# Norms and logits of the first experts stage moved into the last steps of the attention before it, with one program instead of three

## The reference, cut to what matters

```
x = x + tanh(g_xattn[0]) * L0_xattn(layernorm(x), ctx)
# L0_ffn, on h = layernorm(x):
probs = softmax(h @ Wr.T)                      # 8 experts
top 2 of probs, scaled to sum 1 -> w[t, e]
mid = einsum('ti,eri->ter', h, A)              # rank 16 for each expert
lora = einsum('ter,te,eor->to', mid, w, Bm) * 2.0
x = x + tanh(g_ffn[0]) * (h @ Wb.T + bias + lora)
x = x + tanh(g_xattn[1]) * L1_xattn(layernorm(x), ctx)   # with an RMS norm in front
```

## Time and profile before

| | us |
|---|---|
| median of 3 runs (lowest, highest) | 1671.79 (1670.3, 1673.09) |
| the profiled execution, its own time | 1676.02 |
| span of its trace | 1673.8 |
| last project of the first attention, last matmul starts | 160.63 |
| first logits matmul of the experts stage | 168.20 |
| first dense matmul | 184.49 |
| first kv matmul of the second attention | 220.99 |

### The profile page before, as it was taken

How to read it: one execution, slowest core, us unless ns; L and a number is a source line. 1 busy time by engine, 2 the same in 40 slices (tenths; PEclk the granted TensorE clock), 3 DMA queues, 4 the chain that set the end, 5 groups by cost and what they waited for, 6 DMA issues and landing times.

```text
span 1673.8 us, 25566 instructions
## 1 busy us (share of the span) xinstructions
PE 1552.4 (93%) x8786; PEld 1231.5 (74%) x8786; DVE 900.1 (54%) x1793; ACT 699.6 (42%) x2010; POOL 633.3 (38%) x602
## 2 busy tenths in 40 slices
PE   5897978988879999999999999899899999999998
PEld 4664766657668888888888887677677777777775
DVE  5786557858831221222222223688666766776666
ACT  4443244436435444543444344553334434333442
POOL 3543135466433231331323132334544444454430
PEclk9998999989999999999999999899999999999998
DMA  5000111011120110101001010104321212212001
GB/s 208 1 2 25 52 45 38 1 57 68 45 76 26 39 51 1 64 15 37 26 27 51 1 51 30 59 34 112 93 72 51 89 39 77 64 54 74 29 14 51
DMA packets 27885, 81.41 MB, mean 49 GB/s; under 512 B 3248, under 2 KB 11952, under 8 KB 22768
## 3 DMA queue, kind: packets, MB, share of 16 engines
q1 hardware_dynamic: 26896, 79.44, 14.4%
q10 hardware_dynamic: 864, 0.30, 0.1%
HBM read 69.25 MB, written 10.49 MB: 48 GB/s over the span
## 4 chain that ended last, share of the span: by engine, by line
PE 52%; issue 12%; DVE 4%; POOL 3%; ACT 1%; POOLq 0%; DVEq 0%; ACTq 0%
PE bank L397 32%; PE bank L1296 7%; PE bank L1284 2%; PE pair L2082 2%; PE bank L2060 2%; PE pair L1265 2%; POOL wo_low L388 1%; PE pair L397 1%; PE bank L1273 1%; POOL wq_low L1021 1%; PE bank L2068 1%; POOL probs L1030 1%; DVE probs L1914 0%; DVE out_low L1944 0%; DVE small L222 0%
## 5 line engine op out<-in xcount | busy, mean ns | idle before, releaser
L397 PE MATMUL bank<-hid_high,wq_high 128*128 128x512 f32 (+1 forms) x640 | 257.6, 402 | 1.7 <-issue 1.5
L397 PE MATMUL bank<-hid_high,wq_low 128*128 128x512 f32 (+1 forms) x640 | 239.9, 375 | 0.0
L397 PE MATMUL bank<-hid_low,wq_high 128*128 128x512 f32 (+1 forms) x640 | 238.5, 373 | 0.0
L1206 DVE SCALAR_TENSOR_TENSOR x_stream<-bank,gates,x_stream 128x512 f32<-128x512 f32 x64 | 48.1, 751 | 352.8 <-PE bank L1296 352.8
L1030 POOL TENSOR_TENSOR probs<-probs,small 128x512 f32<-128x512 f32 x64 | 67.1, 1048 | 356.9 <-DVE small L1194 356.9
L1809 ACT ACTIVATE probs<-probs,small 128x64 f32<-128x64 f32 x256 | 86.2, 338 | 135.2 <-DVE small L1933 135.2
L397 PEld LDWEIGHTS bank<-hid_high,wq_high 128*128 128x128 f32 x640 | 122.9, 192 | 25.5 <-issue 4.6
L397 PEld LDWEIGHTS bank<-hid_high,wq_low 128*128 128x128 f32 x640 | 122.7, 192 | 22.8 <-issue 0.2
L397 PEld LDWEIGHTS bank<-hid_low,wq_high 128*128 128x128 f32 x640 | 123.5, 193 | 20.3 <-issue 3.1
L1104 ACT ACTIVATE probs<-pair,small 128x128 f32<-128x128 f32 x256 | 90.5, 366 | 82.8 <-DVE small L1188 80.2
L593 POOL TENSOR_TENSOR probs<-probs,small 128x512 f32<-128x512 f32 x64 | 66.8, 1043 | 127.8 <-DVE small L773 127.6
(11 more groups left out here) (339 smaller groups left out, 4012.7 us busy)
## 6 DMA issues: line engine op xcount, KB each, us to landing
raw_q<-in_L_wq SPq DMA_DIRECT2D x18, 1024.0 KB, 4.9
raw_o<-in_L_wo SPq DMA_DIRECT2D x18, 1024.0 KB, 4.9
values<-ctx_values SPq DMA_DIRECT2D x32, 256.0 KB, 4.0
values_t<-ctx_keys SPq DMA_DIRECT2D x8, 512.0 KB, 3.3
raw_c<-in_L_wkv SPq DMA_DIRECT2D x6, 512.0 KB, 3.5
raw_o<-in_L_wkv SPq DMA_DIRECT2D x5, 512.0 KB, 4.8
x_stream<-in_x SPq DMA_DIRECT2D x8, 256.0 KB, 9.9
ctx_keys<-raw_o SPq DMA_DIRECT2D x8, 256.0 KB, 2.0
```

The lines of the kernel that those rows point to most:

```text
L397: last = k.nc.tensor.matmul(out, stationary(a, c), moving(b, c), start=n == 0, stop=n == total - 1)
L1206: nc.vector.scalar_tensor_tensor(xt, k.bank[7][:], gate, xt, ALU.mult, ALU.add).then_inc(k.x_done, 1)
```

## The change

The blocks of `attention_first`, `experts` and `attention_second` become one block, and `experts` is gone. In its place:

- Within the steps of the first attention: tile t is normalized and transposed in step `DENSE_SLOT[t]` (25, 27, 29, 31, 33, 34, 35 for tiles 0 to 6), and its low part and its logits come one step later. The statistics of tiles 0 to 6 are taken one tile at a time, with POOL's power right in its steps. ACT splits the experts' weights in steps 23 (`wc`) and 24 to 27 (`wq`), POOL in steps 24 and 25 (`wc`) and 26 to 29 (`wq`). The choice among experts for tiles 0 to 3 is in DVE's steps 34 (`choose`) and 36 (`weigh`).
- `dense_tail`: tile 7's norm and logits, the choice for tiles 4 to 7, the dense and second products of all tiles, the updates.
- The second attention follows without a barrier; its weights are fetched as soon as the buffers are free.
- The buffers of `mid`, tables and second weights move to places that the first attention has done with.

```diff
+DENSE_SLOT = {0: 25, 1: 27, 2: 29, 3: 31, 4: 33, 5: 34, 6: 35}
+DENSE_AT = {n: t for t, n in DENSE_SLOT.items()}
...
     # attention16, POOL, step n
+            if not rms:
+                if n == 8:
+                    dense_clear()
+                if n % 4 == 2 and n >= 10:
+                    dense_rstd(n // 4 - 2)
+                if n in (24, 25):
+                    dense_low_c(n - 24)
+                if 26 <= n < 30:
+                    dense_low_q(n - 26)
...
     # attention16, ACT, step n
+            if not rms and n - 2 in DENSE_AT:
+                logits(DENSE_AT[n - 2])
...
+            if not rms:
+                if n == 23:
+                    high_c()
+                if 24 <= n < 28:
+                    high_q(n - 24)
+                if n in DENSE_AT:
+                    high(DENSE_AT[n])
+                if n == 35:
+                    exponent(0)
...
     # attention16, DVE, step n
+            if not rms and n - 1 in DENSE_AT:
+                low(DENSE_AT[n - 1])
+            if not rms and n in DENSE_AT:
+                apply(DENSE_AT[n])
...
+            if not rms and n == 34:
+                choose(0)
+            if not rms and n == 36:
+                weigh(0)
...
     # attention16, PE, end of step n
+            if not rms and n in DENSE_AT:
+                dense_transposes(DENSE_AT[n])
+            if not rms and n - 1 in DENSE_AT:
+                dense_logits(DENSE_AT[n - 1])
...
     # dense_tensor
+    def transposes(t):
         pe.wait_ge(k.route_xn, t + 1)
         if t:
             pe.wait_ge(k.route_lo, t)
...
+    def logits(t):
         pe.wait_ge(k.route_lo, t + 1)
         if t:
             pe.wait_ge(k.route_sbuf, t)
         else:
+            pe.wait_ge(k.lo_c, k.at("lo_c", 4))
...
+    # dense_tail
+    @block.vector
+    def _(dve):
+        tile_stats(7, k.at("x_done", 0))
+        scale_bias(k.at("loaded_const", 0))
+        apply(7)
+        low(7)
+        choose(1)
+        update(0)
+        weigh(1)
+        update(1)
+        next_stats(0)
+        for t in range(2, T):
+            update(t)
+            next_stats(t - 1)
+
+    @block.tensor
+    def _(pe):
+        dense(0)
+        transposes(7)
+        dense(1)
+        gated(0)
+        logits(7)
+        dense(2)
+        second(0)
+        second(1)
+        second(2)
+        dense(3)
+        second(3)
+        gated(1)
+        for t in range(4, T):
+            dense(t)
+            second(t)
...
-def attention_second(k):
-    with k.nc.Block() as block:
+        dense_tail(k, block)
         attention16(k, 1, True, block)
         quant_mlp(k, block)
```

More of the change, by code:

```diff
@@ L567, in _ @@
             ln_rstd_gpsimd(k, pool, p, p + 1 - k.early)
+        for p in range(LATE if rms else 0):
+            ln_rstd_gpsimd(k, pool, p, p - 2)
         last_rstd_gpsimd(k, pool)
@@ L668, in _ @@
         queries(0, 1)
-        for n in range(N + LAG + 1):
+        if not rms:
+            high_c, high_q, high, logits, exponent, gated = dense_scalar(k, act)
+        for n in range(N + LAG + 1 if rms else N + LAG + 2):
             d = n - LAG
+            if not rms and n - 2 in DENSE_AT:
+                logits(DENSE_AT[n - 2])
             if 0 <= d < N:
@@ new lines, in choose @@
+    def choose(b):
+        dve.wait_ge(k.route_sbuf, k.at("route_sbuf", 4 * b + 4))
+        rows = slice(4 * b, 4 * b + 4)
+        top, lg, cut, rep, wgt = (m[n][:, rows] for n in ("top", "lg", "cut", "rep", "wgt"))
+        for t in range(4):
+            last = nc.vector.max(top[:, t, :], lg[:, t, 0:8])
+        chain.step(last)
+        nc.vector.tensor_tensor(wgt, lg[:, :, 0:8], top[:, :, 0:1].broadcast_to([P, 4, 8]),
+                                ALU.subtract).then_inc(k.route_max, 1)
+        chain.step(nc.vector.tensor_copy(cut[:, :, 0:2], top[:, :, 0:2]))
+        for t in range(4):
+            last = nc.vector.match_replace(rep[:, t, :], cut[:, t, :], lg[:, t, :], TAKEN)
+        chain.step(last)
+        chain.step(nc.vector.tensor_tensor(top, rep[:, :, 0:8], lg[:, :, 0:8], ALU.not_equal))
@@ new lines, in weigh @@
+    def weigh(b):
+        rows = slice(4 * b, 4 * b + 4)
+        top, wgt, zs = m["top"][:, rows], m["wgt"][:, rows], m["zs"][:, rows]
+        dve.wait_ge(k.route_exp, k.at("route_exp", b + 1))
+        chain.step(nc.vector.tensor_tensor(wgt, wgt, top, ALU.mult))
+        chain.step(nc.vector.tensor_reduce(zs, wgt, AX, ALU.add))
+        chain.step(nc.vector.reciprocal(zs, zs))
+        chain.step(nc.vector.tensor_scalar(zs, zs, 4.0, None, ALU.mult))
+        chain.step(nc.vector.tensor_tensor(wgt, wgt, bcast(zs, 4, 8), ALU.mult))
+        for t in range(4 * b, 4 * b + 4):
+            last = nc.vector.tensor_tensor(m["hw"][:, t, :].rearrange("p (e r) -> p e r", e=E),
+                                           m["mid"][:, t, :].rearrange("p (e r) -> p e r", e=E),
+                                           bcast(m["wgt"][:, t, 0:E], E, 16), ALU.mult)
+        last.then_inc(k.route_p, 1)
@@ L1583, in second, with dense @@
[L1583 to L1587 removed]
+    def dense(t):
+        pe.wait_ge(k.route_lo, t + 1)
         if t >= 4:
             pe.wait_ge(k.route_done, t - 3)
[L1590 to L1593 removed]
@@ L1596, with gated @@
-ROUTE_BANKS = (0, 1, 6, 7)
+        n = 0
+        for c in range(C):
+            for s, w in PAIRS:
+                nc.tensor.matmul(k.bank[ROUTE_BANKS[t % 4]][:], hid_x(k, s, c, t), k.wq[w][:, c * D:(c + 1) * D],
+                                 start=n == 0, stop=False)
+                n += 1
+    def gated(b):
+        pe.wait_ge(k.route_p, b + 1)
+        for t in range(4):
+            last = nc.tensor.transpose(k.bank[2 + b][:, t * P:(t + 1) * P], m["hw"][:, 4 * b + t, :], k.ident[:])
+        last.then_inc(k.route_wt, 1)
```

394 lines of the change are left out of this document (203 added, 191 removed).

## The result

| | before | after |
|---|---|---|
| median of 4 runs on one chip, us (lowest, highest) | 1671.09 (1670.3, 1673.09) | 1656.90 (1655.67, 1657.73) |
| the profiled execution, its own time | 1676.02 | 1655.67 |
| span of its trace | 1673.8 | 1653.8 |

The ratio is 0.9913, with a 95% interval of 0.9896 to 0.993: 14.2 us less by the medians. Forecast were 1659.3 us and 12.5 less.

What follows compares the result with a forecast made beforehand. PE was taken as the bound from 161.03 to 220.99, DVE as leading loop steps 25 to 31. With 27.5 us less behind the loop and 15.0 more in it, net 12.5 less: median 1671.79 becomes 1659.3, range 1650.5 to 1667.0.

Steps and rivals of the forecast that it cites:

- Behind the loop: From the last project to the first kv product: PE's remaining work and one wait, 34.2 us for 59.96, 25.8 less.
- The second choice: In the tail: choice for tiles 4 to 7, about 6.5 us, lies under 9.0 us of PE's products.
- The kv products' clock: The 48 kv products behind a full PE run at the high clock, 11.1 us for 12.80, 1.7 less.
- (1) S(24) to M(27): Loop: first logits wait for POOL's second low part of `wc`, lower clock follows, M(27) at 138.9; 8.9 us more.
- (2) to the low part of step 31: Loop from M(27): DVE's work of 16.0 us plus waits makes 18.4 for 17.5; 0.9 us more.
- (3) to the update of tile 7: Loop's last steps to the last project's end: PE leads, 16.8 us for 13.6; 3.2 us more.
- lock of DVE and POOL: Loop: seven normalizings held up by POOL's instructions, 7.7 us at worst, nothing at best; 2.0 us more taken.
- the first: Rival, loop: first logits do not hold the loop up; 19 to 20 us less, 1652; chance 0.15 (mostly absent).
- More spells: Rival, loop: two more low-clock spells and worst lock, 4.5 less, 1667; chance 0.15 shared with lock or late start.
- Hand-overs exposed one by one: Rival, loop: each tile's path through four engines uncovered, 9.5 us slower, 1681; decides at 3.2 a tile; slower 0.06.
- The second attention's start: Rival: something else, such as DVE's chain through both norms, sets it; kv hole stays, costing 5.5 us, 1665; 2 in 100.

Runs made afterwards that it cites:

- first trace: The changed kernel's profile from its first measurement against the kernel before; median 1656.90 us, ratio 0.9913.
- second trace: The changed kernel measured and profiled once more, with no edit; median 1657.26 us, ratio 0.9907 to the kernel before.
- the early split: Changed kernel with `wc` split earlier, on POOL in steps 22 and 23 and on ACT in step 22; 1653.55 us, ratio 0.9881.
- the last experiment: Kernel with `wc` split early, `weigh(0)` and tile 6's statistics late, plus PE's logits behind the next step's scores; 1649.03 us, ratio 0.9862.
- the kernel with the border: Changed kernel with a block of its own again for the second attention, starting when the tail has ended on all engines; 1663.70 us, ratio 0.9942.

## Why the prediction was right

**Behind the loop.** Forecast were 34.2 us in place of 59.96; 33.77 were measured to the first kv matmul's start, of them one hole of 1.01 (forecast 0.9), where the prediction had put it. The second choice is hidden; no wait over 1.01 stands in the tail. The forecast also took the high clock there, where the experts stage before had 0.83 over its 16.29 us of logits and transposes; "the rest" ran at 1.00 in every trace of the changed kernel and its variants, but what brought that was not tested.

**The kv products' clock, 1.7 less.** They ran at 1.00 and took 11.50 with the pipeline's ends (forecast 11.1), so the gain over this profile of before is there. That closing the hole brings it is not shown: with the hole back, the products ran at 1.00 too. This term has the right size without its cause.

**The loop.** Its three pieces against the earlier trace rows, for both traces of the changed kernel. Before, they were 11.17 (118.79 to 129.96), 17.48 and 13.62 us:

| piece | forecast | first trace | second trace |
|---|---|---|---|
| (1) S(24) to M(27) | +8.9 | 21.01, +9.8 | 20.36, +9.2 |
| (2) to the low part of step 31 | +0.9 | 18.12, +0.6 | 17.84, +0.4 |
| (3) to the update of tile 7 | +3.2 | 18.06, +4.4 | 16.68, +3.1 |
| lock of DVE and POOL | +2.0 | in the above | in the above |
| sum | +15.0 | +14.9 | +12.6 |

(1) The mechanism is shown by the early split: with the low part made in time the wait goes from 7.51 to 1.74. The forecast had M(27) at 138.9, and it came at 138.83, the logits taking 2.70 (2.6) and the transpose and S(27) 2.15 (1.8). That date is a little lucky: S(24) was 0.97 us earlier than before, and counted from it the piece is 0.9 longer than forecast, half of it ahead of the logits.

(3) A spell at the low clock, absent in the second trace, made 1.4 of the 4.4 in the first. Without it the piece is the forecast one. The wait that the prediction named, tile 5's transposes behind DVE's other work in step 34, is the 1.98 at 166.07.

**The mis-sized term is the lock, 2.0 us.** Normalizing in the changed kernel at L1749, over all eight:

```profile
L1749 DVE TENSOR_SCALAR ctx_staging<-x_stream,small x8: 498/540/798, 122.8 to 179.6; 128x512 f32<-128x512 f32 x8
```

The seven in the loop were to lose 0.3 us each. None lost more than 0.26, and with a mean of 603 ns against the median of 540 they lost about 0.4 together. The step that failed is the one from "POOL works half of the time" to a wait of half an instruction at every other start. Only two of the seven began while POOL was at a product, at 122.84 and 145.67, both half a microsecond before it ended. A third, at 165.47, began 0.12 us before the end of one of POOL's powers and took 0.54, no longer than the others. POOL was busy 21.30 of the loop's 52.99 us, not half of it, and it waits for the sums of DVE in each step, so that the two are not placed at random to each other. The term also left out the other direction: three of POOL's products that began beside a normalizing took 1.22 to 1.25 us instead of 1.04, 0.6 together, and the one at 130.38 stands ahead of the low part that the first logits wait for. With 0.4 in place of 2.0 the forecast of the loop would have been 13.4, and the two traces, 12.6 and 14.9, lie on both sides of it. That the forecast sum of 15.0 meets the 14.9 of the first trace is luck: the three pieces without the lock were forecast at 13.0, and they measured 14.9 with the 0.4 in them, of which 0.9 more is in piece (1) and 1.4 is a spell of the clock in piece (3) that comes and goes.

**The sum.** Loop and rest together give 12.6 us less in the first trace (116.77 to 104.20) and 14.9 in the second; the runs say 14.2 and, the second time, 16.0 (1673.24 to 1657.26). The span of the profiled execution was 20.0 shorter than that of before. Of the 7.4 beyond these stretches 1.0 lies ahead of S(24), and 6.5 behind the transposes, where the same 7786 matmuls kept PE busy 1353.27 us instead of 1363.07; in the second trace only 1.3 lies there. The slices with a lower PEclk stand at other places of the page in each run, and the profile of before was of an execution 4.2 over its median. So taking the sum from the median, as the prediction did, was the right choice.

**The rivals.** The hold-up was there, so the first fell; made true by moving the split, it gave 1653.55, where 1652 was forecast for it. More spells: beyond the one behind the first wait, one of 1.4 us in the first trace and none in the second. Hand-overs exposed one by one: behind the first wait PE waits once for a tile's low part (1.60 us) and once for its normalizing (1.98), not 3.2 us at each tile, and by the last experiment the waits at low parts lie beside DVE's work. The second attention's start: its kv products follow the last second product at once.

## What to carry to other kernels

When a product is moved into a loop that runs in order, find for each operand the engine that makes it last and what stands ahead of it in that engine's list. Here a weight split placed two steps too late, behind two products that waited for DVE, stopped every engine and took back 6.7 us of trace, and moving it cost nothing that the trace shows. The move itself was nearly free where PE had gaps: six tiles' logits cost 11.6 us in a stage that PE bounds and at most some 2.4 in a loop where DVE is almost as busy as it. And profile one kernel twice, and compare the granted clock of the two stretches, before a difference of 2 us between two traces is given a cause.

## What the runs showed of the hardware

The same program with the same wait of 7.51 us got a clock of 0.57 in the 6.77 us behind it in one execution, and 0.75 in the 6.71 us behind it in another. Behind the same wait of 1.98 us (tile 5's transposes) the clock was 0.64 over 3.93 us in the first trace of the changed kernel, and 1.00 in the second. The first trace ahead of the end of that wait and behind it:

```profile
157.43:166.07 8.64, 6.66 (x46) 5.31 (x46) 5.46 (x14) 2.83 (x7) 2.63 (x4) 1.00 0.51 183
166.07:170.00 3.93, 3.93 (x25) 2.89 (x26) 2.50 (x17) 1.01 (x4) 0.00 (x0) 0.64 0.00 0
```

A hole of 3.18 us before the kv products left the clock at 1.00, one of 3.82 in the profile of before was followed by 0.87. A spell at the low level behind a short hole can thus come or stay away in the same program. The long stop of 7.5 us was followed by one in all three traces that have it (in the kernel with the border the mean was 0.79 over 6.90 us).

Where normalizing on VectorE and a product on GpSimd met, the one that began second was slowed: at 130.38 POOL's product began 0.16 us behind the normalizing and took 1.24 instead of 1.04; at 145.67 normalizing began 0.51 us before POOL's product ended and took 0.80 instead of 0.54, and POOL's next, begun meanwhile, took 1.22. Over the eight traces of the changed kernel and its variants, normalizings that began 0.45, 0.51, 0.57 and 0.60 us before the end of POOL's product took 0.74, 0.80, 0.85 and 0.88 us: 0.28 or 0.29 more than what was left of it each time. One begun 0.12 us before the end of POOL's short power took 0.54, as with nobody beside it. The Trainium skill (SBUF — State Buffer, "Who interferes with whom") describes an exclusive lock between the two; these rows agree with it, for what is left of the other's instruction comes back in full in the length of the second. The loss against 0.54 is what is left less some 0.26, up to 0.34 us here, and not a whole instruction (1.04). In the kernel before, where four of POOL's low parts of 1.28 to 1.48 us followed each other, a normalizing took 1.64.
